# The dense branches of groups 0 to 2 at the end of the second routing of a two-mixture attention kernel

## What is computed

```python
x = x + _L0_attn_a_ref(_layernorm(x), ...)
x = x + _L0_ffn_ref(_layernorm(x), ...)
x = x + _L0_attn_b_ref(_layernorm(x), ...)
x = x + _L0_ffn_ref(_layernorm(x), ...)
...
# _L0_ffn_ref: D = 256, E = 8 experts, K = 2 of them for each token, hidden 512
abel_out = _gelu(xn @ abel_w + abel_b)
logits = xn @ moe_gate_w + moe_gate_b
topw, topi = jax.lax.top_k(logits, K)
topw = jax.nn.softmax(topw, axis=-1)
h = _gelu(jnp.einsum('bsd,edh->ebsh', xn, ew1) + eb1[:, None, None, :])
eo = jnp.einsum('ebsh,ehd->ebsd', h, ew2) + eb2[:, None, None, :]
moe_out = jnp.einsum('ebsd,bse->bsd', eo, w_dense)
for i in range(NROT):
    moe_out = moe_out @ expm(gens[i])
gate = jax.nn.sigmoid(jnp.concatenate([abel_out, moe_out], axis=-1) @ gc_w + gc_b)
return residual + abel_out * (1.0 - gate) + moe_out * gate
```

## Time and profile before

| | us |
|---|---|
| median of 3 runs | 1418.49 (1414.60 to 1419.76) |
| the profiled execution, its time | 1422.55 |
| the profiled execution, its span | 1420.9 |
| PE busy | 1180.7 (83%) |
| DVE busy | 862.8 (61%) |
| ACT busy | 495.4 (35%) |
| POOL busy | 411.6 (29%) |
| PE's share of the chain that ended last | 52% |
| mean granted clock of PE | 0.917 of full speed |

### The profile page before, as it was taken

The page is one execution under the profiler, slowest core; times in us unless marked ns, Lnnn a source line. Parts: engine busy times, 40 slices in busy tenths (PEclk is TensorE's granted clock), DMA queues, the critical chain, the costliest instruction groups (busy, mean ns, idle before and its releaser), DMA issues.

```text
span 1420.9 us, 26058 instructions
## 1 busy us (share of the span) xinstructions
PE 1180.7 (83%) x7280; PEld 1022.1 (72%) x7281; DVE 862.8 (61%) x2756; ACT 495.4 (35%) x967; POOL 411.6 (29%) x480
## 2 busy tenths in 40 slices
PE   6796876955599999992699998999883799999958
PEld 5664555854488989992588987888772688998947
DVE  6435766744456666665676658766536456666646
ACT  1111551332244444441233333343342334444435
POOL 3001101566134444441000000104454244444420
PEclk9897995877899999996899999999896799999989
DMA  9400231446474333335011011001157663343357
GB/s 288 145 0 7 83 119 52 153 149 215 152 237 120 90 91 89 91 87 208 0 46 45 1 45 46 1 1 56 71 217 244 198 226 103 105 135 103 106 173 249
DMA packets 75727, 161.73 MB, mean 114 GB/s; under 512 B 11302, under 2 KB 36594, under 8 KB 75642
## 3 DMA queue, kind: packets, MB, share of 16 engines
q1 hardware_dynamic: 55082, 105.45, 21.5%
q0 software_dynamic: 19776, 54.45, 12.5%
q10 hardware_dynamic: 784, 0.79, 0.2%
HBM read 88.92 MB, written 71.73 MB: 113 GB/s over the span
## 4 chain that ended last, share of the span: by engine, by line
PE 52%; issue 12%; DVE 6%; DMA 3%; ACT 3%; another core or an unknown queue 3%; POOL 3%; POOLq 1%; SPq 1%; DVEq 0%; ACTq 0%
PE bank L2077 15%; PE bank L1621 6%; PE bank L1622 6%; PE bank L1490 6%; PE bank L1623 6%; PE bank L1647 3%; PE bank L1700 2%; DMA xh<-slots_in 2%; PE bank L2135 2%; POOL xh L1301 2%; PE bank L1630 2%; PE bank L1533 1%; PE bank L186 1%; POOLq L1300 1%
## 5 line engine op out<-in xcount | busy, mean ns | idle before, releaser
L1621 PE MATMUL bank<-ew,rows 128*128 x852 | 298.4, 350 | 4.3 <-DVE rows L1175 2.6
L1622 PE MATMUL bank<-low_in,rows 128*128 x852 | 273.3, 321 | 0.0
L1623 PE MATMUL bank<-ew,rows 128*128 x852 | 272.8, 320 | 0.0
L1312 POOL DMA_INDIRECT results<-xh x142 | 141.8, 998 | 295.7 <-DVE xh L1203 277.5
L1621 PEld LDWEIGHTS bank<-ew,rows 128*128 128x128 f32 x852 | 161.8, 190 | 15.3 <-issue 8.2
L1623 PEld LDWEIGHTS bank<-ew,rows 128*128 128x128 f32 x852 | 161.4, 189 | 12.2
L1622 PEld LDWEIGHTS bank<-low_in,rows 128*128 128x128 f32 x852 | 162.5, 191 | 6.0
L1457 ACT ACTIVATE xh<-bank 128x512 f32<-128x512 f32 x142 | 85.0, 599 | 219.4 <-PE bank L1623 219.4
L1212 DVE TENSOR_TENSOR rows<-bank,rows 128x512 fp32r<-128x512 f32 x142 | 98.3, 692 | 96.1 <-ACT rows L198 82.1
L1291 POOL DMA_INDIRECT slots_in<-xh,work x120 | 117.1, 976 | 101.2 <-DVE work L1071 67.6
L634 POOL TENSOR_TENSOR work<-work,mhalf 128x8 f32<-128x8 f32 (+1 forms) x22 | 38.7, 1760 | 332.7 <-DVE work L627 332.6
(11 more groups left out here) (334 smaller groups left out, 2037.5 us busy)
## 6 DMA issues: line engine op xcount, KB each, us to landing
xh<-slots_in POOLq DMA_DIRECT2D x142, 129.0 KB
low_in<-low SPq DMA_DIRECT2D x32, 512.0 KB
xh<-results SPq DMA_DIRECT2D x14, 1032.0 KB, 5.2
residual<-xs SPq DMA_DIRECT2D x16, 512.0 KB
dense<-ab SPq DMA_DIRECT2D x16, 512.0 KB
xs<-residual SPq DMA_DIRECT2D x16, 512.0 KB
ab<-dense SPq DMA_DIRECT2D x9, 512.0 KB, 9.3
xs<-in_L_attn_a_x_dram SPq DMA_DIRECT2D x4, 1024.0 KB
```

Of the source, the lines that this page charges most:

```text
L1312: pool.indirect_dma_start(out=yg, out_offset=bass.IndirectOffsetOnAxis(ap=back[j % RING], axis=0), in_=yr[j % RING], in_offset=None).then_ ...
L1621: pe.matmul(o, hi, f32r(high(c)), start=(c == 0), stop=False)
L1622: pe.matmul(o, hi, f32r(low(c)), start=False, stop=False)
L1623: last = pe.matmul(o, lo, f32r(high(c)), start=False, stop=(stop and c == chunks[-1]))
```

## The change

The order of the steps in the second mixture becomes [3, 4, 5, 6, 7, 0, 1, 2]. With it move the totals' matmul (`total_rows`, now right behind the rank of group 7, with the dense matmuls of steps 4 to 7 still to come), one gate on DVE (three instead of four are among the choices), the semaphores of the spills (counted by step rather than by group), and the two early weight loads: in the second mixture all eight experts are fetched behind the blank writes, the first two of them ahead of the wait for the fourth tile of slots. The first mixture is as before.

```diff
-            ORDER = [3, 0, 4, 1, 5, 2, 6, 7] if r == 1 else list(range(NG))
+            ORDER = [*range(EARLY_GROUPS, NG), *range(EARLY_GROUPS)]
...
-                LATE = {NG - 4: (0,), NG - 3: (1,), NG - 2: (2, 3)} if r == 0 else {NG - 3: (0,), NG - 2: (1,), NG - 1: (2, 3)}
+                LATE = {NG - 4: (0,), NG - 3: (1,), NG - 2: (2, 3)} if r == 0 else {NG - 3: (0,), NG - 2: (1,), NG - 1: (2,)}
...
-                for p in range(NG // 2, NG):
+                for p in range(NG // 2 if r == 0 else NG // 2 - 1, NG):
                     dense_gate(ORDER[p])
...
                     sp.wait_ge(res_ok, GT * (g + 1))
-                    sp.dma_start(xs_out[g], xs[:, tiles(g), :].rearrange("p t c -> p (t c)")).then_inc(spilled[g % 4], 16)
+                    sp.dma_start(xs_out[g], xs[:, tiles(g), :].rearrange("p t c -> p (t c)")).then_inc(spilled[p % 4], 16)
                     sp.wait_ge(gelu_ok, p + 1)
...
-                    sp.wait_ge(spilled[e % 4], 32 * (e // 4 + 1 if r == 0 else 2))
+                    sp.wait_ge(spilled[step_of[e] % 4], 32 * (step_of[e] // 4 + 1 if r == 0 else 2))
                     sp.wait_ge(zab_ok, GT * (step_of[e] + 1))
...
                     spill(p)
-                    if 0 <= p - (3 if r == 0 else 5) < EARLY:
-                        fetch_weights(p - (3 if r == 0 else 5))
+                    if r == 0 and 0 <= p - 3 < EARLY:
+                        fetch_weights(p - 3)
...
                     sp.dma_start(xg[bass.ds(at, P), :], zero[:]).then_inc(padded, 16)
                 for n in range(1, LATE_FOLDS):
                     store_fold(n)
+                for e in range(EARLY if r == 1 else 0):
+                    fetch_weights(e)
                 sp.wait_ge(x_ld[RING - 1], 16)
...
+                def total_rows():
+                    pe.wait_ge(run_ok, NG)
+                    pe.wait_ge(lg_ok, NG)
+                    pe.matmul(bank[:, 6, 0:E], onesb[:], run[NG % 2], start=True, stop=True).then_inc(rank_ps, 1)
+
...
                     if p == 1:
                         dense(0)
+                    if p == NG - EARLY_GROUPS and r == 1:
+                        total_rows()
```

More of the change, by code:

```diff
@@ L977, in mixture @@
             EARLY_GROUPS = 3 if r == 1 else 0
-            ORDER = [3, 0, 4, 1, 5, 2, 6, 7] if r == 1 else list(range(NG))
+            ORDER = [*range(EARLY_GROUPS, NG), *range(EARLY_GROUPS)]
             step_of = {g: p for p, g in enumerate(ORDER)}
-            assert all(step_of[g] < step_of[g + 4] for g in range(NG - 4))
             if r == 0:
@@ L1319, in spill @@
                     sp.wait_ge(res_ok, GT * (g + 1))
-                    sp.dma_start(xs_out[g], xs[:, tiles(g), :].rearrange("p t c -> p (t c)")).then_inc(spilled[g % 4], 16)
+                    sp.dma_start(xs_out[g], xs[:, tiles(g), :].rearrange("p t c -> p (t c)")).then_inc(spilled[p % 4], 16)
                     sp.wait_ge(gelu_ok, p + 1)
-                    sp.dma_start(ab_out[g], ab[:, tiles(g), :].rearrange("p t c -> p (t c)")).then_inc(spilled[g % 4], 16)
+                    sp.dma_start(ab_out[g], ab[:, tiles(g), :].rearrange("p t c -> p (t c)")).then_inc(spilled[p % 4], 16)
                 def fetch_weights(e):
                     after(sp, low_ld, WEIGHTS * e)
-                    sp.wait_ge(spilled[e % 4], 32 * (e // 4 + 1 if r == 0 else 2))
+                    sp.wait_ge(spilled[step_of[e] % 4], 32 * (step_of[e] // 4 + 1 if r == 0 else 2))
                     sp.wait_ge(zab_ok, GT * (step_of[e] + 1))
@@ L1593, in tensor @@
                     turn_late(1)
-                pe.wait_ge(run_ok, NG)
-                pe.wait_ge(lg_ok, NG)
-                pe.matmul(bank[:, 6, 0:E], onesb[:], run[NG % 2], start=True, stop=True).then_inc(rank_ps, 1)
+                if r == 0:
+                    total_rows()
                 pe.wait_ge(xT_ok, NG)
```

## The result

| | before | changed |
|---|---|---|
| median (20 runs each) | 1417.62 (1413.05 to 1423.80) | 1427.49 (1413.57 to 1432.20) |
| ratio to before, 95% interval | 1 | 1.0063 (1.0049 to 1.0078) |
| the profiled execution, its time | 1422.55 | 1423.56 |

The changed kernel is 0.6% slower; the forecast was 0.8% faster. The two profiled executions lie at different places of their spreads and differ by 1.0 us only, so I compare stages, not totals.

What follows compares the result with a forecast made beforehand. The prediction took the second routing's chain of waits through SP's queue, not PE, to set the first `up`: 12 us earlier, less 1 us in the tile loop, takes the 1418.49 us median to 1407.5, range 1399 to 1415.

Steps and rivals of the forecast that it cites:

- The stage and its bound: Tile loop, bound by PE, keeps its length; second routing is a chain of waits, and the change is inside it.
- The 1 us charged to the loop: Tile loop: expert 1's weights load beside the first tiles, whose fetches land later; 1 us lost, bounds 0 and 3.
- The dense chain: Second routing: dense work on PE ends at 1076.6 as before, with the same 5.9 us of stalls; last Gelu about 1077.6.
- POOL: Second routing's scatters: back to back from group 4 at 1038.5, ending at 1079.5 instead of 1094.0, 14.5 us earlier.
- SP: SP's queue: last spill issued at 1077.7, blank writes start at 1078.3 instead of 1085.85, done at 1089.5 instead of 1101.8.
- Weights and rows: Before the first `up`: rows allow 1097.7, expert 0's weights land at 1096.4 to 1098.6; 1098 taken, 12 us earlier.
- The sum: Whole kernel: 12 us from an earlier first `up`, less 1 us in the tile loop, a gain of 11 us.
- B: Rival, 17%: stalls grow as scatters run beside the dense chain; one long wait leaves a 5 us gain, 1413.5 us.
- A: Rival, 20%: without early weight loads the second routing's stalls shrink too, first `up` at 1092, 1401.5 us.
- C: Rival, 5%: expert 0's late weight load becomes the bound before the first `up`; 9.3 us slower, 1427.8 us.

Runs made afterwards that it cites:

- hold_three: Changed kernel with the second routing's scatters of groups 4 to 7 held until the last Gelu; one run, 1426.7 us where the kernel before took 1416.9.
- hold_four: Changed kernel with the second routing's scatters of groups 4 to 7 held until the last Gelu, timed with intervals; ratio 1.0106 to the kernel before.
- hold: Changed kernel with the second routing's scatters of groups 4 to 7 held until the last Gelu, first run; ratio 1.0148 to the kernel before.
- after_four: Changed kernel, unchanged, timed again where TensorE's signals come late; ratio 1.0083 to the kernel before.
- after_again: Changed kernel, unchanged, second trace, on a chip without late signals; one run, 1363.2 us where the kernel before took 1371.6.
- late_weights: Kernel before, in its old order of groups, with the weights of experts 0 and 1 both issued behind the blank writes; ratio 1.0005 to it.
- early: Changed kernel with the blank writes ahead of the last two groups' spills and four more steps' dense gates earlier on DVE; ratio 0.9961 to the kernel before.

## Why the prediction was wrong

- *The stage and its bound.* Right: the tile loop kept its length (262.8 for 263.8), and all was decided in the second routing. The 1 us charged to the loop, for tile fetches beside expert 1's weights, didn't show.
- *The dense chain: "with the same 5.9 us of stalls".* **This is the step that failed.** The last Gelu was to end at 1077.6 and ended at 1094.2, 16.6 us late, though the stage began 2.4 us earlier (1013.73 for 1016.11). I had called the stalls a constant of the stage. In the trace before, three groups' scatters (3, 4, 5) and three of group 6's lay beside the chain and group 7's behind it; the change puts all five beside it. hold_three and hold_four show that it is the scatters beside it: with those held back the chain ends at 57 us on a late chip. On prompt chips the step holds nearly as forecast: the last Gelu comes 55.0 to 55.8 us after the last attention rows, against 52.7 before, 2 to 3 us later.
- *POOL.* Group 3's scatters were forecast at 1023.1 and came at 1020.73, group 4's at 1038.5 and came at 1037.12. "Back to back" was not so on the late chip: pauses of 3.28 and 4.23 us, since the ranks came late as well. The last scatter ended at 1084.88, not 1079.5: 9 of the 14.5 us, and 6.7 counted from the start of the stage.
- *SP.* Right but for the start: its first step is at 1094.6 instead of 1078.3, as the last spill waits for the Gelu. By then POOL was done, so none of the writes was slow: 9.0 us for the eight, where the forecast had 11.2. The last landed after 3.11 us (2.57 forecast).
- *Weights and rows.* Right: expert 0's weights took 7.39 us (6.92 to 9.06 forecast) and came within half a us of the rows. With 16.6 us of Gelu added, the forecast's own sum gives a first `up` at 1098 + 16.6 = 1114.6; it was 1113.51. The one term carries the error; behind it the shorter blank writes (-2.2) and a slower first fetch (3.73 us for 2.36) nearly cancel.
- *The sum.* Gain 11 us forecast; on prompt chips it is 8.4 to 11.1 us (1361.21 for 1369.62, 1360.46 for 1371.58, 1363.16 for 1371.58), on late ones a loss of 9.9 and 10.9 us (1427.49 for 1417.62, 1427.74 for 1416.88).
- *The rivals.* B was the right mechanism, late signals on ACT and PE ahead of the last Gelu, from the earlier trace rows, and its sign that would show it (waits of 7 us or more) is there: 8.99 us on ACT and 7.85 on PE, beside 8.56 on DVE. It was given 17% and sized by one wait of 10.58 us, of which it took 8; there are several, and they cost the chain 19 us against before. A, fewer stalls without the weights' traffic, was the wrong way round. C didn't happen: the first `up` waited for rows. That C's price, 1427.8, is the measured 1427.49 is chance. "Slower" was given 5% and only to C; by B's own sum a second such wait turns its gain of 5 us into a loss of 3 and a third into one of 10, so B should have had a chance there.

## What to carry to other kernels

A wait that the profile can't name ("remote", or a releaser that had long been done), and that ends shortly after a series of scatters, can be a cost of what runs beside it; holding that back, as in hold, is the test. Such a cost moves with the scatters, so never carry it over as a constant when the change moves them. Place a block of scatters where the engines that exchange signals with PE have none due, as beside one long product, and release it by the signal that begins that product. Time an order on more than one chip: here the sign of the change depends on which one it was.

## What the runs showed of the hardware

- There are chips on which TensorE's signals reach ScalarE and VectorE up to 10.6 us late (changed kernel; 14.0 in after_four) while GpSimd issues indirect DMAs in series, and chips on which the same instructions see none of it (0.01 us, after_again). The kernel before takes 46 us more there, 3.4%, of which 24 and 9 lie in its two routings. Some late signals came out within a series, others 1.7 to 2.5 us after its end, several at once. Some signals due within a series weren't late (due 1052.33 and 1079.71 in the changed kernel). Single indirect DMAs, one to a tile in the tile loop, cost nothing of the kind: the second mixture's loop takes 263.8 us on the one and 263.0 on the other. What the chips differ in, and whether it is the signal that is late or the matmul's last write, stays open; nothing that would tell was tried. Every time here is of an execution whose span and clock were recorded, so whether recording plays a part isn't shown either.
- A write of blank rows costs SP's queue 1.09 us alone. Beside scatters it costs 3.6 and 5.0 us from start to start on a late chip (late_weights) but 1.0 to 2.6 in hold_three, on that same chip, and 1.1 to 1.4 on a prompt chip (8 in 8.80 us in early). A scatter takes 1.09 to 1.18 us instead of 0.96 in part of such stretches, on both kinds of chip.
